# A graph network on one core: histogram, ranking and the dense first layers as one interleaved program, with one power for both norms

## What is computed

```python
h = elu(concat(x[row], edge_attr) @ W1a + b1a) @ W1b + b1b
agg = segment_sum(h, col) / maximum(counts, 1)
x = layernorm(x + (elu(concat(x, agg) @ W2a + b2a) @ W2b + b2b))      # layer 0
inv = rsqrt(degree + 1)
x = layernorm(x + (segment_sum((x * inv)[col], row) + x * inv) * inv @ W.T)   # layer 1
```

## Time and profile before

| | |
|---|---|
| median of 3 runs | 5338.57 us (5330.03 to 5353.4) |
| the profiled execution | 5351.75 us, of which 5349.9 us are the profile's span |
| mean granted TensorE clock | 0.831 of full speed |
| busy over the whole span | PE 3501.4 us, DVE 3446.6, ACT 1939.1, POOL 3496.5 |
| histogram | 36.3 to 137.8 us |
| ranking | 137.8 to 785.6 us |
| lists | 785.6 to 817 us |
| dense layers | 817 to 1448 us |
| first edge stage | 1448 to 1990 us |

### The profile page before, as it was taken

How to read it: one execution, slowest core, us unless ns; L and a number is a source line. 1 busy time by engine, 2 the same in 40 slices (tenths; PEclk the granted TensorE clock), 3 DMA queues, 4 the chain that set the end, 5 groups by cost and what they waited for, 6 DMA issues and landing times. The chain is left out here.

```text
span 5349.9 us, 63884 instructions
## 1 busy us (share of the span) xinstructions
PE 3501.4 (65%) x14784; PEld 2211.3 (41%) x14784; DVE 3446.6 (64%) x10282; ACT 1939.1 (36%) x4034; POOL 3496.5 (65%) x3880
## 2 busy tenths in 40 slices
PE   4443437888668884222999999689788858681025
PEld 3343325666535552111555554344344447561002
DVE  7555637888645553332788888555576659796764
ACT  0000005878623332111777777222222222223532
POOL 0666656888756754775788888544268867454667
PEclk9677768999889985555999999799898879896568
DMA  1212124555423322221333333333333248683544
GB/s 31 65 43 50 44 48 142 173 172 173 132 61 86 90 75 54 60 56 53 107 125 125 126 126 115 105 107 105 91 96 97 87 139 245 166 194 125 179 160 119
DMA packets 422477, 581.32 MB, mean 109 GB/s; under 512 B 69157, under 2 KB 191708, under 8 KB 422268
## 3 DMA queue, kind: packets, MB, share of 16 engines
q1 hardware_dynamic: 361660, 495.02, 29.5%
q0 software_dynamic: 54912, 83.37, 7.4%
q10 hardware_dynamic: 5696, 0.55, 0.1%
HBM read 370.70 MB, written 211.65 MB: 109 GB/s over the span
## 5 line engine op out<-in xcount | busy, mean ns | idle before, releaser
L1114 PE MATMUL ps<-big,Whh 128*128 128x512 f32 x1176 | 540.0, 595 | 34.5 <-DVE big L1132 31.2
L649 PE MATMUL ps<-big,hid 128*128 128x256 f32 x832 | 235.5, 448 | 299.7 <-remote 222.3
L866 POOL TENSOR_TENSOR rstd<-vareps,mhalf 128x4 f32<-128x4 f32 x392 | 429.9, 1109 | 0.0
L1060 ACT ACTIVATE hid<-ps,b 128x512 f32<-128x512 f32 x196 | 117.9, 674 | 803.9 <-PE ps L1004 803.9
L1525 PE MATMUL ps<-big,We 128*128 128x512 f32 x800 | 373.4, 622 | 2.7 <-issue 1.7
L649 PEld LDWEIGHTS ps<-big,hid 128*128 128x128 f32 x832 | 188.3, 230 | 349.8 <-issue 317.4
L669 POOL DMA_INDIRECT meta<-me,rank_ix x208 | 214.4, 1031 | 160.1 <-DVE rank_ix L623 97.6
L1114 PEld LDWEIGHTS ps<-big,Whh 128*128 128x128 f32 x1176 | 211.8, 190 | 255.2 <-issue 252.2
L661 POOL DMA_INDIRECT me<-node_tab,ix x208 | 205.3, 987 | 163.8 <-ACTq L569 100.7
L1147 POOL TENSOR_TENSOR big<-big 128x512 f32<-128x512 f32 x196 | 251.7, 1304 | 44.3 <-ACT big L1141 44.3
L1673 DVE SCALAR_TENSOR_TENSOR big<-r2N,zN 128x512 f32<-128x512 f32 x400 | 257.6, 696 | 34.0 <-issue 26.7
(11 more groups left out here) (378 smaller groups left out, 10801.4 us busy)
## 6 DMA issues: line engine op xcount, KB each, us to landing
xN<-x_tab SPq DMA_DIRECT2D x196, 256.0 KB, 2.7
x_tab<-zN SPq DMA_DIRECT2D x173, 256.0 KB, 5.2
h_tab<-yN SPq DMA_DIRECT2D x124, 256.0 KB
krow<-key_row SPq DMA_DIRECT2D x100, 256.5 KB
agg<-in_xt SPq DMA_DIRECT2D x98, 256.0 KB, 3.9
agg<-x_tab SPq DMA_DIRECT2D x98, 256.0 KB
xN<-in_x SPq DMA_DIRECT2D x97, 256.0 KB, 2.7
x_tab<-big SPq DMA_DIRECT2D x96, 256.0 KB, 4.8
```

Source lines behind the costliest of these rows:

```text
L649: last = nc.tensor.matmul(PS[2 * k + j // 2][:, (j % 2) * LO:(j % 2 + 1) * LO], hid2[q][k][:, h, j * P:(j + 1) * P], R[:, k, h, :], start= ...
L866: nc.gpsimd.tensor_tensor(self.rs[u][:, :, 0], self.ve[u][:, :, 0], mhalf[:, 0:J], ALU.pow).then_inc(self.rstd, 1)
L1114: last = nc.tensor.matmul(bank[:, :], Whh[:, l, c * D:(c + 1) * D], h, start=True, stop=not both)
```

## The change

The blocks of the histogram, the ranking and the dense layers become one block. A table `plan`, made when the program is built, gives the order of their steps, and every engine follows it (`follow`):

- 26 histogram steps, with a dense step after each second one;
- the table, and two dense steps;
- 112 quarters of ranking groups (`quarters` splits a group's work in four), with 90 dense steps spread over them.

A dense step k does a part of several groups: the hidden layer of group k, the output of k - 1, first norm's statistics of k - 2, its scaling of k - 3, second product of k - 4, second statistics of k - 5, second scaling of k - 6. The statistics of both norms (128x8) go through one `eps` add and one `shift` on VectorE and one power on GpSimd. The piece of `inv_e` is now made in the first edge stage, 25 pieces of 128x9. The ranking has PSUM banks 0 to 3, the dense layers 4 to 7: one buffer for the hidden layer, one bank for outputs, one for transposes and the second product. All of it, the dense layers too, is written out and has no loop. The lists stage comes after. What is computed is as before.

```diff
-INV_STEP = -(-2 * ET // NPAIR)
+INV_STEP = -(-2 * ET // EGR)
...
+HB, OUT0, TURN = PS[4:6], PS[6], PS[7]
+xd = [*x2N[0], spare_x]
+xt = [agg[u][:, h, :] for u in range(2) for h in range(2)]
+hid1 = hid2[0]
+x1T = [hid2[1][1][:, h, :] for h in range(2)]
+r1, r2 = rN, r2N
+x1, x2 = [*yN, x2N[1][0]], [*zN, x2N[1][1]]
...
+bias = [b0[:, 4 + h:5 + h] for h in range(2)]
+spans = [slice(j * P, (j + 1) * P) for j in range(J)]
+LAST = NG + 7
...
+plan = []
+taken = 0
+for i in range(EG):
+    plan.append(("hist", i))
+    if i % 2:
+        plan.append(("dense", taken))
+        taken += 1
+plan += [("table", 0), ("dense", taken), ("dense", taken + 1)]
+taken += 2
+slots, left, begun = J * (EG + 2), LAST - taken, taken
+for n in range(slots):
+    plan.append(("rank", n))
+    while taken - begun < -(-(n + 1) * left // slots):
+        plan.append(("dense", taken))
+        taken += 1
+assert taken == LAST
+def follow(**steps):
+    for name, n in plan:
+        if name in steps:
+            steps[name](n)
+def quarters(at, *, first=(), second=(), third=(), fourth=()):
+    i, s = divmod(at, J)
+    for lag, step in (first, second, third, fourth)[s]:
+        staged(i - lag, EG, step)
...
+    def dense(k):
+        staged(k + 1, NG, load_x)
+        staged(k + 2, NG, load_xt)
+        staged(k - 4, NG, store1)
+        staged(k - 7, NG, store2)
...
+    def note(i, j):
+        t = i * J + j
+        for f, which in ((4, IX_SRC), (8, IX_DST)):
+            nc.gpsimd.indirect_dma_start(me[:, t, f:f + 4], None, node_tab, at_index(which, i, j)).then_inc(noted[i % 2].sem, 16)
...
+    def place(i, j):
+        after2(pool, noted, i, 32 * J)
+        pool.wait_ge(ranked, 2 * i + 2)
+        t = i * J + j
+        for k in range(2):
+            nc.gpsimd.indirect_dma_start(meta[k], bass.IndirectOffsetOnAxis(ap=rank_ix[:, k, t:t + 1], axis=0),
+                                         me[:, t, :], None).then_inc(stored[k].sem, 16)
...
+    def rank(at):
+        i, s = divmod(at, J)
+        if 0 <= i + 1 < EG:
+            if i >= 1:
+                after2(pool, noted, i - 1, 32 * J)
+            note(i + 1, s)
+        if 0 <= i - 2 < EG:
+            place(i - 2, s)
+    def add_bias(g):
+        after_ring(pool, x_in, g, 16)
+        after(pool, r1d, g - 2)
+        nc.gpsimd.tensor_tensor(flat(xb[g % 2]), flat(xd[g % 3]), flat(b2b_bc), ADD).then_inc(xbd, 1)
+    def power(k):
+        after(pool, epsd, k)
+        after(pool, shd, k - 2)
+        after(pool, x1d, min(k - 4, NG - 1))
+        after(pool, x2d, min(k - 7, NG - 1))
+        nc.gpsimd.tensor_tensor(rsq[k % 2][:, :], veq[k % 2][:, :], mhalf[:, 0:2 * J], ALU.pow).then_inc(powd, 1)
+    def dense(k):
+        staged(k - 1, NG, add_bias)
+        power(k)
...
+    def rank(at):
+        quarters(at, second=((1, look(1)),), fourth=((0, count_group), (0, look(0))))
+    def hidden(g):
+        after_ring(pe, xt_in, g, 16)
+        after(pe, elud, g - 1)
+        for h in range(2):
+            last = nc.tensor.matmul(HB[h][:, :], W2a[:, 0, h * P:(h + 1) * P], xt[g % 4], start=True, stop=True)
+        last.then_inc(hidd, 1)
...
+    def out0(g):
+        after(pe, elud, g)
+        after(pe, r1d, g - 1)
...
+    def dense(k):
+        staged(k, NG, hidden)
+        staged(k - 4, NG, turn1)
+        staged(k - 1, NG, out0)
+        staged(k - 4, NG, out1)
+    follow(hist=hist, table=table, rank=rank, dense=dense)
...
+    def exps(g):
+        after(act, hidd, g)
+        after(act, y1d, g - 2)
+        for h in range(2):
+            last = nc.scalar.activation(hid1[g % 2][:, h, :], HB[h][:, :], ACT.Exp, bias=bias[h])
+        last.then_inc(expd, 1)
...
+    def dense(k):
+        staged(k, NG, exps)
+        staged(k - 4, NG, copy1)
+        staged(k - 3, NG, scale1)
+        staged(k - 6, NG, scale2)
+    follow(dense=dense)
...
+    def rank(at):
+        quarters(at, first=((1, extract(0)), (0, compare(0))), second=((0, compare(1)),), third=((1, extract(1)), (0, match(0))),
+                 fourth=((1, finish_rank), (0, match(1))))
+    def shift(k):
+        q = k % 2
+        after(dve, powd, k)
+        after(dve, x1d, min(k - 4, NG - 1))
+        after(dve, x2d, min(k - 7, NG - 1))
+        nc.vector.scalar_tensor_tensor(of2(shq[q]), of3(mvq[q])[:, :, :, 0], -1.0, of2(rsq[q]), MUL, MUL).then_inc(shd, 1)
...
+    def eps(k):
+        q = k % 2
+        after(dve, mvd, k)
+        after(dve, powd, k - 2)
+        nc.vector.tensor_scalar(of2(veq[q]), of3(mvq[q])[:, :, :, 1], EPS, None, ADD).then_inc(epsd, 1)
+    def elu_low(g):
+        after(dve, expd, g)
+        nc.vector.tensor_scalar(hid1[g % 2][:, :, :], hid1[g % 2][:, :, :], 1.0, -1.0, MIN, ADD).then_inc(tmin, 1)
+    def elu_high(g):
+        after(dve, tmin, g)
+        for h in range(2):
+            last = nc.vector.scalar_tensor_tensor(hid1[g % 2][:, h, :], HB[h][:, :], bias[h], hid1[g % 2][:, h, :], ADD, MAX)
+        last.then_inc(elud, 1)
+    def dense(k):
+        if k:
+            shift(k - 1)
+        staged(k - 5, NG, residual2)
+        staged(k - 2, NG, residual1)
+        staged(k - 5, NG, stats2)
+        staged(k, NG, elu_low)
+        staged(k - 2, NG, stats1)
+        moments(k)
+        staged(k, NG, elu_high)
+        eps(k)
...
-        place(i)
-        staged(i + 2, EG, note)
-    for k in range(2):
-        landed(pool, stored[k], EG * J * 16)
...
+    def inverse_root(g):
+        piece = inv_e[:, INV_STEP * g:INV_STEP * (g + 1)]
+        nc.gpsimd.tensor_tensor(piece, piece, mhalf[:, 0:INV_STEP], ALU.pow).then_inc(rooted, 1)
...
-dense_first()
```

562 lines of the change are left out of this document (258 added, 304 removed).

## The result

The changed kernel takes 5204.89 us (median of 4 runs, 5202.28 to 5211.8), the kernel before 5334.3 us in the same comparison: a ratio of 0.975 (95% interval 0.973 to 0.978), 129 us less. Forecast were 5130 us and a range of 5045 to 5235. The direction and the range hold; the gain is six tenths of the 204 us between 5334 and the forecast.

The account below looks back on a forecast made before the run. Ranking was taken as bound by waiting (294 of 647.8 us a stall after GpSimd DMA runs), the dense stage as evenly full. Three stages 1380.3 to 1163 (-217), edges +8: some -210, 5142 profiled, 5130 median; range 5045 to 5235.

Parts of the forecast that it names:

- slow rhythm: Ranking: matmuls 1.4 us apart after 13 to 17 GpSimd DMAs in a row; 22.6 us lost per two groups, 294 in all.
- The sum of the three stages: Histogram, ranking and dense layers, merged: 1163 us against 1380.3 before, 217 less.
- VectorE ... I take 5.7: VectorE's time for one dense step, 5.7 us; with a ranking quarter of 3.2, 8.9.
- next to no hindrance: Ranking: GpSimd's DMAs beside a busy VectorE take 1.05 us each, against 1.031 and 0.987 over the stage.
- rival B: Merged stage: VectorE's instructions hold up GpSimd, its step 10.9 us; +183 us, 5313 in all; chance 0.05.
- The single hidden buffer costs nothing more: Merged dense steps: one hidden buffer adds no time, as its next use waits for the step before anyway.
- fourth quarters: Ranking quarters where VectorE waits 2.1 us for the exponential, some 21 times: 44 us, and 20 more for the clock.
- rival D: Merged stage: the engines' orders interlock, 2 us more in each of 105 steps; gain gone, 5340 us; chance 0.05.
- rival A: Ranking: the slow rhythm survives, caused by GpSimd's DMAs over time, not run length; +84 us, 5415; chance 0.07.
- the 12 that did no harm in the first edge stage: Runs of 12 GpSimd DMAs there show no slow rhythm; the new order has at most eight in a row.
- The edges' powers: First edge stage: 25 GpSimd powers on inv_e, 44 us, mostly covered by waits; between 0 and 44, taken as 8.
- C: Merged stage: TensorE stays at the half clock, 1524 us instead of 1163; +361, 5490 in all; chance 0.03.

Follow-up runs that it names:

- apart: The changed kernel with the same steps run one after the other instead of overlapped; 5347.6 us, 1.041 of the kernel before on the same chip.
- small_bias: The changed kernel with GpSimd's output bias add cut from 128x512 to 128x8 from the third group on; 5109.8 us, 0.959 of the kernel before.
- res_early: The changed kernel with both residual adds of a dense step moved on VectorE ahead of the next ranking quarter; 5028.5 us, 0.979 of the kernel before.
- before2: The kernel before, unchanged, profiled again on another chip; 5137.7 us, ratio 1.000.

## Why the prediction was right, and where it was off

**What was luck.** The time fell into the range on a chip with the slow rhythm. There some 60 of the 129 us come from the ranking's rhythm, which costs 78 us there and not the 294 that the prediction took, and 26 from the edge stages, for which a small loss was forecast. On an even chip the same change gains 20 us of the 210, a tenth. The mechanism, work of one stage in the waits of the other, is shown by apart; its size was overestimated.

**The sum of the three stages** (forecast 1163, measured 1262.5). GpSimd's terms hold: the power on 128x8 takes 1.69 us (I took 1.65), the DMAs come 1.3 us apart. Off by 100 us are VectorE's terms, in two steps.

*"VectorE ... I take 5.7"* a dense step. Elu's first step takes 1.18 us instead of 0.68: 98 x 0.5 = 49 us. This is the step "next to no hindrance", read from GpSimd's side alone. small_bias shows that its removal is worth more than 49. It is rival B with the engines' parts exchanged.

*"The single hidden buffer costs nothing more"*, and 2.1 us waited only in 21 fourth quarters, together with the histogram 26 + 44 + 20 = 90 us. Measured are 156.7 us before elu's first step alone, 67 more; with the 49 that is 116, so that the other terms together came out some 16 us too high. I followed one chain, from the ranking's matmuls to the exponential, and took all other inputs as old. But step k's transposes wait for step k's residual, which frees their one bank. At 620.17 TensorE starts them after 2.88 us of idle, behind VectorE's residual of 619.35; outputs, second product and the next quarter's look-ups follow in order, and the next step's hidden layer only at 628.41:

```profile
620.17 0.95 PE L701 MATMUL ps<-ident,yN 128*128 128x128 f32 x4 [2.88 <-issue]
...
624.95 3.62 PE L682 MATMUL ps<-big,hotrow 128*128 128x256 f32 x16
628.41 1.88 PE L694 MATMUL ps<-agg,W2a 128*128 128x512 f32 x4
```

The exponential follows it,

```profile
630.32 1.27 ACT L732 ACTIVATE hid<-ps,b 128x512 f32<-128x512 f32 x2 [5.49 <-PE ps L694]
```

and elu's first step starts at 631.62 after 3.00 us of idle. res_early breaks this loop, and 87 us go, some 54 of them the loop's (above). It is rival D in small, 1 to 2.5 us in most steps rather than 2 in all. The histogram's 13 pairs have it too: 15.4 to 16.5 us each (the first 14.2), not 14.1.

**What the forecast rested on.** *"294 of the 647.8 us of ranking are the slow rhythm"* was wrong. I took the difference to VectorE's pace, where GpSimd sets it. On an even chip the rhythm is gone and the ranking still takes 564.8 us. The sum was not hurt, as it priced GpSimd's DMAs in each quarter by itself; rival A's 5415 us was (its own +84 on 5338.57 would be 5423). Nor did "the 12 that did no harm in the first edge stage" hold: they do harm in both edge stages on this chip. That the rhythm nearly goes in the merged stage was forecast, but from a premise that the trace of the kernel before already contradicts. In the merged stage the rhythm is nearly gone on the slow-rhythm chip: the last placement ends at 1298.8 us there and at 1280.9 on an even one. The 18 us left are what the rhythm still costs, if nothing else differs between the chips. So some 60 of the change's 129 us are rhythm that the ranking no longer meets.

**The edges' powers** (forecast +8, between 0 and 44). On an even chip 23 to 36 us, as GpSimd is the bound from step 3 on, which its 139.4 us of waits hid: without the slow rhythm the kernel before waits there for 51.9 us only (before2). On the chip of the prediction -26. The sign of the term depends on the chip.

**Rivals.** A: no matmuls 1.4 us apart in a row, which is a weak sign, as the kernel before has them at the place of the earlier trace rows alone; the 18 us above say more, and A's time didn't come. Its cause, the number of DMAs over time, isn't ruled out. B: the lock is there, but it is VectorE that is held up; price 49 us in elu's step, some 85 with all that goes with it, and not 183 on GpSimd. C: the granted clock is 0.83, near the 0.87 taken. D: in part, above.

**The size in sum:** forecast -210, by the profiled executions -146. Merged stages 100 us too optimistic; edges 34 too pessimistic; 64 net.

## What to carry to other kernels

When two in-order programs are merged, follow every single-buffered bank around the loop, from its last reader back to its next writer, for each kind of step: the lag in the plan says how old an input is, not when its output's place comes free. Before an elementwise instruction is left to GpSimd, look at what VectorE runs at that moment: one add of 1.28 us cost as much again on VectorE wherever the two met, and moving it to an engine with idle time brought 24 to 48 us, with a higher granted clock in part of that. A reordering that gains should be read for this too: in res_early a third of the gain was fewer such meetings. And where a time without stalls is taken from one good stretch, check that every engine could keep that pace: VectorE's best group was one that GpSimd could not follow. Last, time the kernel before again beside the change on more than one chip: here the same change was worth 2.5% on one and 0.4% on another.
